# A GNN stack's last network: GpSimd makes set products beside VectorE, fewer sets, two accumulators

## The reference, cut to what matters

```python
x1 = x_nodes[src].reshape(-1, N_SEG, EXTENT)          # 8192 x 16 x 32
x2 = x_edges.reshape(-1, N_SEG, EXTENT)
i1, i2, i3 = (path_indices[:, 0], path_indices[:, 1], path_indices[:, 2])   # 64 paths
contrib = path_coeffs[None, :, None] * x1[:, i1, :] * x2[:, i2, :]
edge_out = jnp.zeros((x2.shape[0], N_SEG, EXTENT)).at[:, i3, :].add(contrib)
out = jnp.zeros((n_nodes, OP_SIZE)).at[dst].add(edge_out.reshape(-1, OP_SIZE))
# and at the end: x = x + out
```

## Time and profile before

| | before |
|---|---|
| device time, median of three (us) | 840.88 |
| the profiled execution: its time, its span (us) | 840.28, 838.5 |
| mean granted TensorE clock | 0.989 |
| TensorE busy (us, share) | 784.4, 94% |
| VectorE busy | 601.4, 72% |
| ScalarE busy | 220.0, 26% |
| GpSimd busy | 126.9, 15% |
| the last network's groups begin at (us from the span's start) | 532, 579, 637.4, 697.9, 758.4 |

### The profile page before, as it was taken

How to read it: one execution, slowest core, us unless ns; L and a number is a source line. 1 busy time by engine, 2 the same in 40 slices (tenths; PEclk the granted TensorE clock), 3 DMA queues, 4 the chain that set the end, 5 groups by cost and what they waited for, 6 DMA issues and landing times.

```text
span 838.5 us, 11005 instructions
## 1 busy us (share of the span) xinstructions
PE 784.4 (94%) x3172; PEld 530.8 (63%) x3172; DVE 601.4 (72%) x1575; ACT 220.0 (26%) x458; POOL 126.9 (15%) x150
## 2 busy tenths in 40 slices
PE   6889999999898999999999999889999999999978
PEld 3557667667566666667567564566686685685753
DVE  8776676675686544453553563789999999999995
ACT  7623123123121311311311312403404304305200
POOL 5000000000101000000000001611441361441000
PEclk9999999999999999999999999899999999999989
DMA  4912333323131433333342100751632443330000
GB/s 167 347 63 102 113 103 110 113 82 131 63 134 64 162 113 126 119 113 121 118 146 80 63 1 25 228 173 51 200 102 80 138 134 104 111 88 0 1 0 25
DMA packets 39335, 88.39 MB, mean 105 GB/s; under 512 B 3986, under 2 KB 4319, under 8 KB 39295
## 3 DMA queue, kind: packets, MB, share of 16 engines
q1 hardware_dynamic: 34656, 72.72, 25.4%
q0 software_dynamic: 4640, 15.21, 6.1%
HBM read 86.86 MB, written 1.05 MB: 105 GB/s over the span
## 4 chain that ended last, share of the span: by engine, by line
PE 74%; DVE 14%; issue 5%; DVEq 3%; ACT 2%; POOL 1%; ACTq 0%; another core or an unknown queue 0%; POOLq 0%
PE PS L764 44%; PE PS L1085 15%; PE PS L1071 11%; DVE big L1539 2%; PE PS L773 2%; DVE tail L1530 1%; PE PS L936 1%; DVE x L1602 1%; PE PS L885 1%; DVEq L1502 1%; PE PS L799 1%; DVEq L1506 1%; DVE big L1226 1%; PE PS L981 1%; DVE big L1276 1%
## 5 line engine op out<-in xcount | busy, mean ns | idle before, releaser
L764 PE MATMUL PS<-big 128*128 128x512 f32 (+1 forms) x368 | 137.1, 524 | 1.7 <-DVE big L1430 1.7
L1530 DVE SCALAR_TENSOR_TENSOR tail<-big,coef 128x448 f32 (+3 forms) x208 | 125.2, 614 | 5.0 <-issue 4.7
L1539 DVE TENSOR_TENSOR big<-big,tail 128x448 f32 (+3 forms) x208 | 115.3, 554 | 3.6 <-DVE tail L1530 2.4
L764 PEld LDWEIGHTS PS<-big 128*128 128x128 f32 x368 | 67.4, 190 | 63.4 <-issue 54.8
L764 PE MATMUL PS<-hT,big 128*128 128x256 f32 (+1 forms) x512 | 87.0, 329 | 4.4 <-ACT hT L687 4.4
L585 POOL DMA_INDIRECT big<-h_rows,src_i x58 | 75.1, 1295 | 83.4 <-PE PS L1071 60.8
L764 PEld LDWEIGHTS PS<-hT,big 128*128 128x128 f32 x512 | 77.5, 191 | 15.2 <-ACT hT L687 7.3
L555 POOL TENSOR_TENSOR rstd<-var,minus_half 128x1 f32<-128x1 f32 x34 | 20.5, 605 | 409.9 <-DVE var L1136 409.8
L1071 PE MATMUL PS<-big,hotd_more 128*128 128x512 f32 x152 | 66.0, 592 | 0.0
L1085 PE MATMUL PS<-hotd_more,tail 128*128 128x256 f32 x280 | 64.6, 386 | 0.0
L1085 PEld LDWEIGHTS PS<-hotd_more,tail 128*128 128x128 f32 x280 | 54.6, 195 | 7.9
(11 more groups left out here) (210 smaller groups left out, 1110.1 us busy)
## 6 DMA issues: line engine op xcount, KB each, us to landing
big<-in_edge_attr_dram SPq DMA_DIRECT2D x32, 512.0 KB, 3.5
big<-in_L_gnn_vn_W_dram SPq DMA_DIRECT2D x12, 1024.0 KB, 5.4
big<-in_L_gnn_m_w_dram SPq DMA_DIRECT2D x8, 1024.0 KB, 5.3
big<-in_L_gnn_gcn_W_dram SPq DMA_DIRECT2D x7, 1024.0 KB, 5.2
big<-in_L_gnn_wv_dram SPq DMA_DIRECT2D x4, 1024.0 KB, 5.3
big<-in_L_gnn_wq_dram SPq DMA_DIRECT2D x4, 1024.0 KB, 5.0
big<-in_L_gnn_wk_dram SPq DMA_DIRECT2D x4, 1024.0 KB, 5.1
big<-in_L_gnn_wo_dram SPq DMA_DIRECT2D x4, 1024.0 KB, 5.3
```

The source lines that it names most:

```text
L764: return pe.matmul(o, lhsT, rhs, start=start, stop=stop)
L1530: dve.scalar_tensor_tensor(out=prod[:, slot, tiles, :], in0=xs[:, tiles, bass.ds(i1, EXT)], scalar=coef[:, row:row + 1], in1=xe[:, tiles, ...
L1539: dve.tensor_tensor(o, o, prod[:, slot, tiles, :], ALU.add)._wait_ge(path_step, max(product_at[slot], added_at[0])).then_inc(path_step, 1)
```

## The change

GpSimd makes the products of most sets (`POOL_SETS`): the odd ones of group 0, and all but the first of the other groups; VectorE makes the rest. GpSimd loads the twelve registers of a set itself, waits for the same buffers (`set_used`), and counts in a semaphore of its own, `pool_ready`, which TensorE waits for at these sets, and SP, ScalarE and GpSimd where they reuse a group's buffers. The sets of the groups become 8, 6, 5, 5, 4, so each middle group has four summed rows more. On GpSimd, a group is now: zero, the first set, the gathers of the next group, each waiting for its own tile of `tile_summed`, then the other sets. Group 0 interleaves four gathers between sets. ScalarE zeroes `h` in group 2, and the 32 final pieces go alternately into x and h, each waiting for the one two before; two adds join h to x. A memset of one PSUM region goes away.

```diff
-SETS_OF = [8, 7, 6, 6, 4]
+SETS_OF = [8, 6, 5, 5, 4]
+POOL_SETS = [(1, 3, 5, 7), (1, 2, 3, 4, 5), (1, 2, 3, 4), (1, 2, 3, 4), (1, 2, 3)]
...
             for g in range(2, GROUPS):
                 sp.wait_ge(path_step, STEP_AT[g - 1])
+                sp.wait_ge(pool_ready, POOL_AT[g - 1])
                 edge_group(g)
...
+            def make_set(g, i):
+
+                k, at, n = SETS - SETS_OF[g] + i, SET_AT[g] + i, SIZES[g]
+                pool.load(places, path[0:1, 3 * BLOCK_ROWS * k:3 * BLOCK_ROWS * k + 3 * 4])
+                if at >= 2:
+                    pool.wait_ge(set_used, at - 1)
+                for q in range(4):
+                    i1, i2 = (pool.snap(r, min_val=0, max_val=(SEGS - 1) * EXT) for r in places[3 * q:3 * q + 2])
+                    ins = pool.tensor_tensor(prods[at % 2][:, 0:n, q * EXT:(q + 1) * EXT],
+                                             part[SOURCE_AT[g]][:, 0:n, bass.ds(i1, EXT)],
+                                             part[EDGE_AT[g]][:, 0:n, bass.ds(i2, EXT)], ALU.mult)
+                ins.then_inc(pool_ready, 1)
...
-            fetch_sources(1)
+            for j in range(3):
+                fetch_source(1, j)
+            pool.wait_ge(setcoef_set, 1)
+            pool.wait_ge(picked_kept, BY_PE)
+            group_in(0)
+            for n, i in enumerate(POOL_SETS[0]):
+                make_set(0, i)
+                for j in range(3 + 4 * n, min(3 + 4 * (n + 1), SIZES[1])):
+                    fetch_source(1, j)
             for g in range(1, GROUPS):
                 pool.wait_ge(path_step, STEP_AT[g])
+                pool.wait_ge(pool_ready, POOL_AT[g])
                 zero_sums(g)
+                group_in(g)
+                make_set(g, POOL_SETS[g][0])
                 if g + 1 < GROUPS:
-
-                    pool.wait_ge(tile_summed, START[g])
-                    fetch_sources(g + 1)
+                    for j in range(SIZES[g + 1]):
+                        pool.wait_ge(tile_summed, min(START[g - 1] + j + 1, START[g]))
+                        fetch_source(g + 1, j)
+                for i in POOL_SETS[g][1:]:
+                    make_set(g, i)
...
                 act.wait_ge(path_step, STEP_AT[g])
+                act.wait_ge(pool_ready, POOL_AT[g])
                 zero_sums(g)
+                if g == 2:
+                    act.wait_ge(h_kept, 16 * NT)
+                    act.wait_ge(picked, BY_PE)
+                    act.activation(h[:].rearrange("p t d -> p (t d)"), zero.to_broadcast([P, NT * D]),
+                                   ACT.Copy).then_inc(spare_zero, 1)
...
-                pe.wait_ge(set_ready, n + 1)
+                if i in POOL_SETS[g]:
+                    pe.wait_ge(pool_ready, POOL_AT[g] + POOL_SETS[g].index(i) + 1)
+                else:
+                    pe.wait_ge(set_ready, OWN_AT[g] + sum(o not in POOL_SETS[g] for o in range(i)) + 1)
...
-                if j == 2:
-                    dve.wait_ge(picked_kept, 2)
-                    dve.memset(set_bank(3), 0.0).then_inc(picked_kept, 1)
...
+                    makes = has_set and k - (SETS - SETS_OF[g]) not in POOL_SETS[g]
+                    if makes:
                         while waiting:
                             add_product(*waiting.pop(0))
                         set_rows(k, rows)
...
-                    o = x[:, :, bass.ds(bounded(set_regs[4 * k + q]), EXT)]
-                    link(dve.tensor_tensor(o, o, turned[:, :, q * EXT:(q + 1) * EXT], ALU.add))
+                    n = 4 * at + q
+                    if n >= 2:
+                        dve.wait_ge(placed, n - 1)
+                    o = (h if q % 2 else x)[:, :, bass.ds(bounded(set_regs[4 * k + q]), EXT)]
+                    dve.tensor_tensor(o, o, turned[:, :, q * EXT:(q + 1) * EXT], ALU.add).then_inc(placed, 1)
+            dve.wait_ge(placed, 4 * SETS)
+            for t in range(NT):
+                ins = dve.tensor_tensor(x[:, t, :], x[:, t, :], h[:, t, :], ALU.add)
+            link(ins)
```

More of the change, by code:

```diff
@@ L37 @@
 SETS = PATHS // BLOCK_ROWS
-ORDER = [[0, 1, 2, 3, 4, 5, 6, 7], [1, 2, 0, 3, 4, 5, 6, 7], [2, 0, 3, 1, 4, 5, 6, 7], [2, 0, 3, 1, 4, 5, 6, 7],
+ORDER = [[0, 1, 2, 3, 4, 5, 6, 7], [2, 0, 3, 1, 4, 5, 6, 7], [3, 0, 4, 1, 5, 6, 7, 2], [3, 0, 4, 1, 5, 6, 7, 2],
          [4, 0, 5, 1, 6, 2, 7, 3]]
-SETS_OF = [8, 7, 6, 6, 4]
+SETS_OF = [8, 6, 5, 5, 4]
+POOL_SETS = [(1, 3, 5, 7), (1, 2, 3, 4, 5), (1, 2, 3, 4), (1, 2, 3, 4), (1, 2, 3)]
+POOL_AT = [sum(map(len, POOL_SETS[:g])) for g in range(len(POOL_SETS) + 1)]
 SUMMED_OF = [PATHS - 4 * n for n in SETS_OF]
@@ L44 @@
 SET_AT = [sum(SETS_OF[:g]) for g in range(GROUPS + 1)]
+OWN_AT = [SET_AT[g] - POOL_AT[g] for g in range(GROUPS + 1)]
 STEP_AT = [2 * sum(SUMMED_OF[:g]) for g in range(GROUPS)] + [2 * sum(SUMMED_OF) + 2 * SPLIT_ROWS]
@@ L329, in gnn_stack_kernel @@
             sem, ["h_ready", "hot_squared", "hotd_ready", "acc_zero", "path_step", "tile_summed", "final"])
+        spare_zero, placed = sem("spare_zero"), sem("placed")
+        pool_ready = sem("pool_ready")
         node_summed = sem("node_summed")
@@ L579, in zero_sums, with fetch_source, group_in @@
                 pool.memset(part[SUM_AT[g]][:, ZERO_CUT:SIZES[g], :], 0.0).then_inc(acc_zero, 1)
[L581 to L587, removed]
+            def fetch_source(g, j):
+                tile = START[g] + j
+                pool.indirect_dma_start(out=part[SOURCE_AT[g]][:, j, :], out_offset=None, in_=h_rows,
+                                        in_offset=bass.IndirectOffsetOnAxis(ap=src_i[:, tile:tile + 1], axis=0)
+                                        ).then_inc(x1_in[g], 16)
+            places = [pool.alloc_register(f"place{i}") for i in range(3 * 4)]
+            def make_set(g, i):
[9 more added lines that the diff above has]
+                ins.then_inc(pool_ready, 1)
+            def group_in(g):
+                pool.wait_ge(x2_in[g], 16 * (SIZES[g] // PIECE))
+                pool.wait_ge(x1_in[g], 16 * (SIZES[g] - (0 if g else BY_PE)))
             pool.wait_ge(alpha_done, 2)
@@ L1085, in sum_set @@
                     ins = pe.matmul(set_bank(SETS - SETS_OF[g] + i), prods[n % 2][:, j, :], hotd(j),
-                                    start=g == 0 and j == 0 and SETS - SETS_OF[g] + i != 3, stop=True,
-                                    skip_group_check=True)
+                                    start=g == 0 and j == 0, stop=True, skip_group_check=True)
                 ins.then_inc(set_used, 1)
@@ L1497, in _, with load_block @@
             loads = []
-            def load_block(k):
+            def load_block(g, k):
                 into = regs[len(loads) % 2]
                 loads.append(k)
-                dve.load(into, path[0:1, 3 * BLOCK_ROWS * k:3 * BLOCK_ROWS * (k + 1)])
+                lo = 3 * 4 if k - (SETS - SETS_OF[g]) in POOL_SETS[g] else 0
+                dve.load(into[lo:], path[0:1, 3 * BLOCK_ROWS * k + lo:3 * BLOCK_ROWS * (k + 1)])
                 return into
@@ L1573, in _ @@
                         if behind is not None:
-                            loaded = load_block(behind)
+                            loaded = load_block(*behind)
                     if g == GROUPS - 1 and at >= len(ORDER[g]) - 2:
-                        if behind is not None and not has_set:
-                            loaded = load_block(behind)
+                        if behind is not None and not makes:
+                            loaded = load_block(*behind)
                         split += [(BLOCK_ROWS * k + i, rows[i]) for i in range(4 if has_set else 0, BLOCK_ROWS)]
@@ L1583, in _ @@
                         summed_row(BLOCK_ROWS * k + i, every, *rows[i])
-                        if i == 5 and behind is not None and not has_set:
-                            loaded = load_block(behind)
+                        if i == 5 and behind is not None and not makes:
+                            loaded = load_block(*behind)
                 for tiles in (slice(0, SPLIT_TILE), slice(SPLIT_TILE, n)):
```

11 lines of the change are left out of this document (6 added, 5 removed).

## The result

The changed kernel takes 869.34 us (median of 4 runs, 868.40 to 870.77) where the kernel before takes 841.38 beside it: ratio 1.0337, 95% interval 1.0312 to 1.0361. It is 3.4% slower. Its profiled execution took 868.40 us with a span of 866.6, so 28.1 us of span are to be explained.

What follows compares the result with a forecast made beforehand. TensorE and VectorE were taken as balanced, so only shortening both chains gains. 840.3 + 29.1 (VectorE's groups) + 2.7 (TensorE's clock) - 0.3 (end) = 871.8, forecast 872 us, range 846 to 890.

Steps and rivals of the forecast that it cites:

- the likeliest case: Whole kernel: mutual holds between GpSimd and VectorE make it slower, 854 to 880 us, chance 0.62.
- The hold: Each GpSimd product stops VectorE for its read time: 0.90, 0.77, 0.65 us at 448, 384, 320 elements.
- The sum by group: VectorE's chain, groups 0 to 4: sets leaving, rows added, holds; net +2.4, +9.3, +7.9, +7.9, +1.6, together +29.1 us.
- The saving of the placements: At the end, 32 placements of 11.46 us perhaps halve, but TensorE's last matmuls hide all but 0.3 us.
- TensorE's clock: At the end, TensorE's clock is granted at half after waiting some 7 us for split rows: +2.7 us.
- GpSimd's chain: Groups of 14 tiles: GpSimd's zeroing, sets and gathers plus TensorE's last set, 59.4 us, 66.2 in group 1, under VectorE's.
- No mutual hold: Rival, all groups: VectorE's f32 operations and GpSimd's products do not hold each other, 813 us, chance 0.12.
- Finely interleaved reads: Rival, all groups: reads interleave, so a product costs VectorE 0.55 us net, 846 us in all, chance 0.13.
- GpSimd's chain as the bound: Rival: GpSimd waits for two VectorE operations between its own, group 1 takes 77.7 us; 882 us, chance 0.13.
- VectorE's second population near 1.5 us: Sign in the profile: some 80 VectorE f32 products and adds near 1.5 us, beside 0.68 and 0.62.
- TensorE's half clock: Sign in the profile: TensorE idle at the end of 14-tile groups, its clock granted at half some times more.
- GpSimd's pitch: Sign in the profile: GpSimd's 80 products come at near 1.5 us pitch.

Runs made afterwards that it cites:

- first, second and third experiment: Changed kernel with GpSimd's products replaced by fills (812.3 us), by copies of one input (828.95 us), or with VectorE's summed rows reading one input from PSUM (804.91 us).
- the rest of the change alone: Kernel before, its sets all on VectorE, plus two accumulators, gathers tile by tile and no PSUM memset: 839.85 us, ratio 1.0003.
- writes alone: Changed kernel with GpSimd's 80 products replaced by fills that read nothing: 812.3 us, ratio 0.9676.
- products that hold no one: Changed kernel, GpSimd's products kept, VectorE's summed rows reading one of two inputs from PSUM: 804.91 us, ratio 0.9588.
- two sets gave back in group 3: Changed kernel with eight of GpSimd's 20 sets returned to VectorE, two in each of groups 1 to 4: 860.33 us.
- an earlier start and a filler of the right length: Kernel before with two accumulators, last group's split behind all sets but two, 16 split rows, 16 filler matmuls: 837.93 us, ratio 0.9983.
- the ring in PSUM: VectorE's products written to a two-slot PSUM ring: 861.07 us on the kernel before with the rest of the change, 862.66 on the changed kernel.

## Why the prediction was right, step by step

- **The forecast**, 872 us, against 869.3: the sign, the mechanism and the likeliest case held. Two errors in the groups partly cancel: the holds came out 2.1 us above what was taken, and all other terms 4.2 below (-41.5 in place of -37.3).
- **The hold.** Taken: 0.90, 0.77 and 0.65 us at 448, 384 and 320 elements, 66.4 in all. Measured: 0.92, 0.76 and 0.72, 68.5 in all. That the hold seen on a one-input bf16 operation would meet the f32 operations with two SBUF inputs was an inference; it is now shown, and so are its conditions by the first, second and third experiment.
- **The sum by group.** Predicted +2.4, +9.3, +7.9, +7.9, +1.6, together 29.1; measured +2.0, +8.1, +7.2, +7.6, +2.1, together 27.0. Each group of 14 tiles came out 0.3 to 1.2 us shorter than forecast; this lies in the terms other than the holds. The fewer sets and additional rows came as forecast: 2.3 us a group, and 6.8 measured for three (846.39 against 839.57). A set that leaves VectorE was put at its products alone in these groups, and it also frees 0.12 us of direct wait and some short gaps; the rest of the 4.2 was not traced.
- **The end.** The saving of the placements was called hidden: measured so, by a ratio of 1.0003 for the rest of the change alone and by VectorE's wait, 4.39 us in the changed kernel. The term that was mis-sized is TensorE's clock: +2.7 with -0.3 was written, and the stretch grew by 1.1. The first sixteen matmuls took 8.53 us there instead of 7.13, 1.4 more, behind an idle time of 8.06 us (granted clock 0.83 from 840.9 to 849.4).
- **GpSimd's chain.** A set was put at 6.8 us with 0.7 for its registers; a set of 14 tiles took 5.54 to 6.26, and between two that follow each other no load shows (617.18 and 5.65 end where the next starts, at 622.79). The fourteen gathers were put at 23 us and took 27.5 in group 1 (589.66 to 617.16), eight of them 1.95 to 1.96 each. The two errors have opposite signs. "Narrowly under" VectorE's was wrong in group 1: TensorE ended its sets at 650.2, 2.7 us after VectorE's rows. It lost nothing that shows, since VectorE still sets the end of group 2, at 715.2.
- **The rivals.** "No mutual hold", 813 us, is near the 812.3 measured with writes alone, in part by luck: GpSimd's writes are shorter (0.47 us) than the products that the rival took, and its gathers slower. With products that hold no one the kernel takes 804.9. Finely interleaved reads fell by the constant steps of 1.46 us. GpSimd's chain as the bound fell by TensorE's waits for L1582 and by the 3.0 us that two sets gave back in group 3.
- **The signs that were named.** VectorE's second population near 1.5 us is there, one for each of GpSimd's 52 products of 448 elements; at fewer elements it is shorter. TensorE's half clock came back some times more. GpSimd's pitch was 1.4 to 1.5 us at 448 elements, 1.3 at 384 and 1.1 at 320. Not as told was the first set of group 0, below.

## What to carry to other kernels

Before work goes from VectorE to GpSimd, count the SBUF inputs on both sides: a product that VectorE makes in 0.55 us cost it 0.90 us when GpSimd made it, and nothing when VectorE's own stream had one input in PSUM. A hold is read from the distance between starts, against the same operation undisturbed; and a buffer that takes away the instruction between a producer and its reader adds a direct wait, 0.12 us each time here, which no busy time shows. And a piece of work that ends beside a longer one on another engine is worth shortening only together with that one: the second accumulator gave nothing alone (1.0003) and 0.17% with an earlier start and a filler of the right length.

## What was not expected of the hardware

- **Reading PSUM was free, a direct wait was not.** VectorE's product with an input from PSUM has 675 ns, as with two from SBUF. An instruction that waits for the one directly before it starts some 0.12 us later than one that doesn't: 0.66 instead of 0.54 us between adds in SBUF, 0.72 instead of 0.59 to 0.60 behind a product in the ring in PSUM.
- **The alternation isn't always there.** In the first set of group 0 of the changed kernel GpSimd ran its four products back to back while VectorE's pair waited (timelines of GpSimd and of VectorE):

```profile
534.62 3.30 POOL L603 TENSOR_TENSOR prods<-big 128x320 f32 x4
```
```profile
534.09 4.65 DVE L1573 SCALAR_TENSOR_TENSOR tail<-big,coef 128x320 f32 x2
```

With the ring in PSUM one VectorE product waited 8.76 us, through eight products of GpSimd's. What decides between alternating and this was not settled.
- **One input holds less than half of two**: 0.33 against 0.90 us.
